# Attention outputs normalised in transposed layout through DRAM, and S^T of two heads into neighbouring banks under one exponential

## What is computed

```python
scores = jnp.einsum('bhqd,bhkd->bhqk', q, k) / jnp.sqrt(jnp.float32(HEAD_DIM))
scores = jnp.where(causal[None, None], scores, neg)
probs = jax.nn.softmax(scores.astype(jnp.float32), axis=-1).astype(x.dtype)
out = jnp.einsum('bhqk,bhkd->bhqd', probs, v)
out = out.transpose(0, 2, 1, 3).reshape(B, S, D_MODEL)
return out @ Wo
```

## Time and profile before

| | |
|---|---|
| three timed runs | 2179.16, 2183.64, 2201.61 us (median 2183.64) |
| profiled execution, own time | 2203.77 us |
| span in its profile | 2202.0 us |
| mean granted TensorE clock | 0.938 |
| TensorE, weight load, VectorE, ScalarE, GpSimd busy | 87%, 42%, 56%, 53%, 41% of the span |

### The profile page before, as it was taken

One profiled execution on the slowest core, in us unless ns is written; L12 is line 12 of the kernel. 1 busy time (PEld: TensorE's weight loads), 2 busy tenths in 40 slices (PEclk: granted clock), 3 DMA queues, 4 the chain that ended last, 5 costly groups with the idle time before them and its releaser, 6 DMA issues.

```text
span 2202.0 us, 37596 instructions
## 1 busy us (share of the span) xinstructions
PE 1912.8 (87%) x12579; PEld 922.6 (42%) x12579; DVE 1236.4 (56%) x2714; ACT 1160.7 (53%) x2592; POOL 904.8 (41%) x1209
## 2 busy tenths in 40 slices
PE   5989999999999999999999999999886888888820
PEld 3544344345444444444444544444332444444410
DVE  3455777656677765658777466787723111222248
ACT  1465577667657766665777766678642122222200
POOL 4744432345442354545433554343214122222248
PEclk9998999999999999999999999999988899999965
DMA  5565332222221122212111122111011999999988
GB/s 179 170 222 172 116 118 84 93 68 92 70 91 53 43 70 71 66 54 85 57 38 37 48 61 61 58 54 38 16 46 34 294 301 283 311 323 293 287 249 289
DMA packets 201642, 280.63 MB, mean 127 GB/s; under 512 B 109783, under 2 KB 109783, under 8 KB 201472
## 3 DMA queue, kind: packets, MB, share of 16 engines
q1 hardware_dynamic: 175152, 239.32, 33.4%
q0 software_dynamic: 24576, 35.07, 6.6%
q10 hardware_dynamic: 1744, 4.06, 0.5%
HBM read 168.85 MB, written 147.46 MB: 144 GB/s over the span
## 4 chain that ended last, share of the span: by engine, by line
PE 62%; DMA 11%; ACT 8%; DVE 7%; issue 5%; SPq 3%; POOL 2%; DVEq 1%; POOLq 1%; ACTq 0%
PE ps L867 11%; PE ps L831 7%; DMA gx<-dispatch_scratch 6%; PE ps L802 6%; ACT pr L1093 5%; PE ps L979 5%; PE ps L851 5%; PE ps L891 5%; PE ps L911 5%; PE ps L1011 3%; PE ps L918 3%; SPq L629 2%; PE ps L933 2%; DVE rmax L1275 2%; DMA qT<-mT 2%
## 5 line engine op out<-in xcount | busy, mean ns | idle before, releaser
L1275 DVE TENSOR_REDUCE rmax<-ps 128x1 f32<-128x512 f32 (+3 forms) x1280 | 735.3, 631 | 251.6 <-PE ps L836 164.3
L1093 ACT ACTIVATE pr<-ps 128x512 f32<-128x512 f32 (+3 forms) x1536 | 623.1, 513 | 169.1 <-PE ps L851 166.8
L831 PE MATMUL ps<-kT,qT 48*128 48x512 f16 (+3 forms) x1536 | 350.4, 337 | 24.5 <-DVE rmax L1275 14.4
L867 PE MATMUL ps<-pr,v_ones 128*32 128x512 f32 (+3 forms) x3072 | 334.7, 527 | 6.9 <-ACT pr L1093 2.8
L1572 POOL TENSOR_SCALAR_AFFINE_SELECT pr<-pr 128x512 f32<-128x512 f32 x256 | 163.8, 642 | 415.3 <-ACT pr L1093 414.7
L851 PE MATMUL ps<-qT,kT 50*128 50x512 f16 (+3 forms) x1536 | 301.7, 338 | 33.5 <-DMA qT<-mT 24.6
L1597 POOL DMA_INDIRECT dispatch_scratch<-x,slot_i x192 | 191.7, 999 | 143.9 <-DVE slot_i L1367 94.9
L1630 POOL DMA_INDIRECT acc_scratch<-eo,etok x64 | 98.8, 1543 | 309.6 <-DVE eo L1417 280.4
L831 PEld LDWEIGHTS ps<-kT,qT 48*128 48x128 f16 x1536 | 106.4, 93 | 274.0 <-ACT pr L1093 93.8
L979 PE MATMUL ps<-gu_sb,gxT 128*128 128x384 f32 x512 | 199.5, 515 | 0.0
L802 PE MATMUL ps<-wqkv_sb,xT 128*128 128x288 f32 (+1 forms) x512 | 181.4, 501 | 4.2 <-ACT xT L1048 4.2
(11 more groups left out here) (147 smaller groups left out, 2596.2 us busy)
## 6 DMA issues: line engine op xcount, KB each, us to landing
gu_sb<-w_gu_dram SPq DMA_DIRECT2D x64, 768.0 KB, 6.6
dn_sb<-w_dn_dram SPq DMA_DIRECT2D x64, 384.0 KB, 8.9
dispatch_scratch<-blank SPq DMA_DIRECT2D x64, 288.5 KB, 4.5
gx<-dispatch_scratch SPq DMA_DIRECT2D x64, 288.5 KB, 5.4
rotated_scratch<-qkv SPq DMA_DIRECT2D x32, 384.0 KB, 2.4
grp<-rotated_scratch SPq DMA_DIRECT2D x32, 384.0 KB, 3.6
xin<-x_dram SPq DMA_DIRECT2D x32, 256.0 KB, 3.2
xres<-x_dram SPq DMA_DIRECT2D x32, 256.0 KB, 2.8
```

Of the source, the lines that this page charges most:

```text
L831: last = pe.matmul(o, qT[it % 2][r:r + SROWS, h // 2, q % QPH * P:(q % QPH + 1) * P], kT[it % 2][r:r + SROWS, kh * HALF:kh * HALF + w], st ...
L867: last = pe.matmul(ps[32 * h:32 * h + 32, bank_of["v", it], c0:HALF], v_ones[it % 2][:, kt, :], pr[k % SLOTS][:, h, 0:HALF - c0], start=kt ...
L1093: act.activation(pr[k % SLOTS][:, h, 0:HALF - c0], ps[:, bank_of["s", it, i, h], 0:HALF - c0], ACT.Exp, scale=factor).then_inc(exp_done, 1)
L1275: dve.tensor_reduce(dst[:, heads[0] % 2, heads[0] // 2:heads[0] // 2 + n, q % QPH], ps[:, bank_of["u", it, u], 0:n * w].rearrange("p (h k) ...
```

## The change

What it does: the outputs of an item stay transposed. The copied bank `raw` (256 KB) is stored to DRAM as it is, and two loads per item bring the value rows into half of a chunk of `anT` and the denominator rows into the same rows of `den`, so that two items fill 128 partitions. VectorE then takes the reciprocal of all 128x512 denominators and multiplies, once for a pair of items, and the output projection reads `anT` directly. `raw_transpose`, `attended_transpose`, `copy_anT` and their waits are gone. S^T of two heads goes into two neighbouring banks, one exponential reads both, and the planner looks for such pairs of banks. Several planner constants are others. The diff, cut to its core (renamed counts and removed tiles are left out):

```diff
-H0 = 0.32
-AHEAD = 4
-RESERVE = 3
+H0 = 0.409
+AHEAD = 3
-ULEAD = -0.186
-ALEAD = 0.066
+ULEAD = -0.628
+ALEAD = 0.047
-CLAG = 0
-CSTEP0 = 0.173
-CSTEP1 = 0.124
+CLAG = 0.057
+CSTEP0 = 0.151
+CSTEP1 = 0.113
...
-                for h in range(REP):
-                    kd = REP * k + h - AHEAD
...
+                for p in range(2):
+                    kd = 2 * k + p - AHEAD
+                    op(s_st, ("st", it, i, p), "pe", n_cols / 2400 + 0.008, t_i,
+                       ("exp", *p_unit(kd // 2), kd % 2) if kd >= 0 else None, ("mr", it), bank=("s", it, i, p))
+                    op(s_exp, ("exp", it, i, p), "act", 0.06 + 2 * n_cols / 1200, t_i, ("st", it, i, p),
+                       ("pv", *p_unit(k - SLOTS)) if k >= SLOTS else None, frees=("s", it, i, p), table="exp")
...
-            op(s_rt, ("rt", it), "pe", 0.45, t_i + 2 * step, ("raw", it), bank=("r", it))
-            op(s_an, ("an", it), "dve", 0.67, t_i + 2.2 * step, ("rt", it), ("as", far) if far is not None else None, frees=("r", it))
-            op(s_as, ("as", it), "sp", 0.06, t_i + 3 * step, ("an", it))
+            op(s_as, ("as", it), "sp", 0.06, t_i + 2 * step, ("raw", it))
+            op(s_nl, ("nl", it), "sp", 0.12, t_i + 3 * step, ("as", it), ("an", it // 2 - 2) if it >= 4 else None,
+               ("wo", it // KVH * QPH - QPH - 1) if it >= 2 * KVH else None)
+            if it % 2:
+                op(s_an, ("an", it // 2), "dve", 1.10, t_i + 5 * step, ("nl", it))
...
-                    need = 1
+                    need = 2 if name[0] == "st" else 1
...
+                    if need == 2:
+                        pairs = [(k, k + 1) for k in free_at if k + 1 in free_at]
+                        if not pairs:
+                            continue
...
+            def store_raw(it):
+                sp.wait_ge(pv_copied, it + 1)
+                sp.dma_start(raw_t[it], raw[it % 2][:]).then_inc(raw_out[it % 2], 16)
+
+            def load_raw(it):
+                sp.wait_ge(raw_out[it % 2], 16 * (it // 2 + 1))
+                if it >= 4:
+                    sp.wait_ge(an_ready, it // 2 - 1)
+                if it >= 2 * KVH:
+                    sp.wait_ge(wo_done, QPH * (it // KVH - 1))
+                rows = slice(ROWT * (it % 2), ROWT * (it % 2) + ROWT)
+                sp.dma_start(anT[it // KVH % 2][rows, it % KVH // 2, :], raw_parts[it, 0]).then_inc(raw_in[it // 2 % 2], 16)
+                sp.dma_start(den[it // 2 % 2][rows, :], raw_parts[it, 1]).then_inc(raw_in[it // 2 % 2], 16)
...
-                pe.matmul(ps[:, bank_of["s", it, i, h], 0:HALF - c0],
-                          kT[it % 2][r:r + BROWS, kt * P:(kt + 1) * P],
-                          qT[it % 2][r:r + BROWS, h // 2, c0:HALF],
-                          start=True, stop=True).then_inc(st_done, 1)
+                for h in range(2):
+                    r = ROWT * h
+                    last = pe.matmul(ps[:, bank_of["s", it, i, pair][h], 0:HALF - c0],
+                                     kT[it % 2][r:r + BROWS, kt * P:(kt + 1) * P],
+                                     qT[it % 2][r:r + BROWS, pair, c0:HALF],
+                                     start=True, stop=True)
+                last.then_inc(st_done, 1)
...
-                pe.wait_ge(anT_copied, n + 1)
+                pe.wait_ge(an_ready, QPH * (n // QPH + 1))
...
-                act.activation(pr[k % SLOTS][:, h, 0:HALF - c0], ps[:, bank_of["s", it, i, h], 0:HALF - c0], ACT.Exp,
+                a, z = bank_of["s", it, i, pair]
+                act.activation(pr[k % SLOTS][:, 2 * pair:2 * pair + 2, 0:HALF - c0],
+                               ps[:, a:z + 1:z - a, 0:HALF - c0], ACT.Exp,
                                scale=factor).then_inc(exp_done, 1)
...
-            def attended(it):
...
-                dve.reciprocal(rden[:], rows[:, :, HD])
+            def attended(pp):
+
+                dve.wait_ge(raw_in[pp % 2], 64 * (pp // 2 + 1))
+                heads = anT[pp // (KVH // 2) % 2][:, pp % (KVH // 2), :]
+                dve.reciprocal(den[pp % 2][:], den[pp % 2][:])
                 dve.drain()
...
+                dve.tensor_tensor(heads, heads, den[pp % 2][:], ALU.mult).then_inc(an_ready, 1)
...
+    raw_d = nc.dram_tensor("raw_scratch", (NI * P, HALF), f32, kind="Internal").ap()
```

More of the change, by code:

```diff
@@ L199, in build @@
                 op(s_stk, ("stk", it, j), "pe", 0.45 * cols / 1024, tpp + (0.3 + 0.05 * j) * dp, ("lo", it),
-                   ("st", far, last_far, REP - 1) if far is not None else None, bank=("k", it, j))
+                   ("st", far, last_far, 1) if far is not None else None, bank=("k", it, j))
                 op(s_stc, ("stc", it, j), "act", 0.05 + cols / 1200, tpp + (0.35 + 0.05 * j) * dp, ("stk", it, j), frees=("k", it, j))
@@ L225, in build @@
                 if diagonal(half, kt):
-                    op(s_mask, ("mask", it, i), "pool", 0.61, t_i, ("exp", it, i, REP - 1))
-                op(s_pv, ("pv", it, i), "pe", 0.04 + n_cols / 600, t_i + 1.2 * step, ("exp", it, i, REP - 1),
+                    op(s_mask, ("mask", it, i), "pool", 0.61, t_i, ("exp", it, i, 1))
+                op(s_pv, ("pv", it, i), "pe", 0.04 + n_cols / 600, t_i + 1.2 * step, ("exp", it, i, 1),
                    ("mask", it, i) if diagonal(half, kt) else None, ("v", it) if i == 0 else None,
-                   ("rt", far) if i == 0 and far is not None else None, bank=("v", it) if i == 0 else None)
@@ L230, in build @@
-            op(s_raw, ("raw", it), "act", 0.48, t_i + 1.2 * step, ("pv", it, NP[half] - 1), ("rt", far) if far is not None else None,
+                   bank=("v", it) if i == 0 else None)
+            op(s_raw, ("raw", it), "act", 0.48, t_i + 1.2 * step, ("pv", it, NP[half] - 1), ("as", far) if far is not None else None,
                frees=("v", it))
-            op(s_rt, ("rt", it), "pe", 0.45, t_i + 2 * step, ("raw", it), bank=("r", it))
-            op(s_an, ("an", it), "dve", 0.67, t_i + 2.2 * step, ("rt", it), ("as", far) if far is not None else None, frees=("r", it))
@@ L340, in run @@
                         continue
-                    if name[0] not in ("st", "pv") and len(free_at) - need + held_s + held_v < RESERVE:
+                    if name[0] not in ("st", "pv") and len(free_at) - need + 2 * held_s + held_v < 3:
                         continue
-                    banks = (min(free_at, key=lambda k: (max(at, free_at[k]), -free_at[k])),)
+                    if need == 2:
+                        pairs = [(k, k + 1) for k in free_at if k + 1 in free_at]
+                        if not pairs:
+                            continue
+                        banks = min(pairs, key=lambda v: (max(at, free_at[v[0]], free_at[v[1]]), -free_at[v[0]] - free_at[v[1]]))
+                    else:
+                        banks = (min(free_at, key=lambda k: (max(at, free_at[k]), -free_at[k])),)
                     at = max([at] + [free_at[k] for k in banks])
```

116 lines of the change are left out of this document (29 added, 87 removed).

## The result

The changed kernel takes 2363.38 us (median of four runs, 2342.64 to 2375.77) against 2187.89 us before (four runs, 2179.16 to 2201.61): 1.0786 times, 95% interval 1.0686 to 1.0887. The forecast was 2139. The profiled execution took 2375.77 us, span 2374.0.

The account below looks back on a forecast made before the run. The prediction took TensorE, 96% busy in the steady attention stage, as the bound. Its terms, -57 - 6 + 37 - 8 - 10 - 1 = -45 us, took the median from 2183.6 to 2139, range 2075 to 2205.

Parts of the forecast that it names:

- Part 3: Stores and loads of the new layout on SyncE's queue: cost taken as 0, as the planner spaces them.
- Part 2: VectorE's reciprocal and product per pair: a 4.3 us block, 1.7 us of it exposed at 0.68 share, +37 us.
- the bound of +96: Upper bound for VectorE's normalisation block: 32 x 3.0 us, bare but for the two score units in hand.
- Part 1: Transposes removed from TensorE: -57 us of chain and -6 us of idle time before them.
- rival C: TensorE's busy time is no bound and other waits fill the holes: about 2184 us, chance 0.16.
- Part 4: Two heads per exponential on ScalarE: -8 us on the path, bounds -43 and +20 to +40.
- Part 5: New planner constants, score units aimed earlier, less TensorE waiting for the transfer into qT: -10 us, bounds 25 either way.
- Part 6: End of the attention stage: last raw copy to first projection 9.5 us (+1.4), later projections -2.5, together -1 us.
- B: VectorE's block holds TensorE at each of 32 pairs: 122 us in place of 37, 2224 us, chance 0.12.

Follow-up runs that it names:

- neither: Changed kernel, same order, with VectorE not waiting for the loads and multiplying by 1 instead of taking the reciprocal: 2188.91 us, stage end 1703.7.
- no_reciprocal: Changed kernel, same order, with VectorE multiplying the denominators by 1 instead of taking their reciprocal: 2248.87 us, ratio 1.0361, stage end 1783.9.
- all_off_pairs: Changed kernel without VectorE's load wait or reciprocal, planner told longer maxima issue and later loads: 2208.29 us, ratio 1.0047, stage end 1721.0.
- all_off: Kernel before plus transposed normalisation only, without VectorE's load wait or reciprocal, planner told longer maxima issue and later loads: 2187.71 us, ratio 0.9988.
- compact: Kernel before plus transposed normalisation, reciprocal on one 128x32 copy spread back through DRAM, planner told measured durations: 2196.57 us, ratio 1.0049, stage end 1735.3.
- other_order: Kernel before with two planner constants moved slightly (ALEAD, CSTEP0), same work in another order: 2208.18 us, ratio 1.0104, stage end 1721.1.
- pairs_only: Kernel before plus S^T in pairs of neighbouring banks, one exponential for two heads and AHEAD 3: 2252.30 us, ratio 1.0421, stage end 1759.0.

## Why the prediction was wrong

- **Part 3, the transfers at 0: the step that failed.** The prediction said that the planner "spaces the two by 2.2 us, hence I take 0". The store landed in 2.0 us by its row; after, the median is 3.1 (4.7 in the chain shown), the load takes 5.9, and the two with their issue 11.2 us. The prediction looked for the cost on SyncE; the larger part fell on VectorE, whose wait for the load it did not price at all. By neither and no_reciprocal it is +80 us of stage, +96 beside the long reciprocal.
- **Part 2, the block: length right, exposure too small.** 4.1 us against 4.3 forecast. The Trainium skill, "VectorE: DVE Perf Modes", section "First, the fixed hardware budget", gives a repeat count of 8, from which 4.4 us were estimated for the reciprocal; it took 3.35, so the reading of that count as 8 cycles per element does not hold here. The slope from the 16-column row stands. But the block costs 78 us of stage and not 37: within the bound of +96, which was the case of two units in hand and no other cover.
- **Part 1, the transposes at -63: nothing was returned.** In neither busy time fell by 50 us and the stage by 4; in all_off_pairs by 34, with the stage 13 later. That is rival C for this part: TensorE 96% busy was not the bound in these orders, as its own waits for others were next. In all_off and compact the step fails in another way, which no rival named: busy time fell by 14 us and not at all, as the other matmuls covered more time. The Trainium skill, "Perfetto Trace Analysis", section "Identifying the Most-Contended Engine", takes weight-load share rather than matmul busy share as the nearer measure. This case is in line with it: 45% of the steady stage, and in neither 50 us off the matmuls bought 4. What spoke against it, that the chain is mostly matmuls, was a poor witness: such a chain names who worked last, not what comes next when that work is gone.
- **Part 4, pairs at -8.** The exponential was sized right (1.02 us for 128x1024 against 1.05), but its saving did not show: +51 alone, outside the bounds of -43 and +40, with longer waits of ScalarE for S^T and of TensorE for banks. On top of the new normalisation pairs and constants gained 24 to 43 us.
- **Part 5, constants at -10 with ±25.** Alone +41, where other_order shows some 13 for a new order as such. The bound of 25 was too narrow, and it was drawn from the waits: they hardly changed, the overlap of the matmuls did.
- **Part 6, the end.** From the last raw copy to the first projection it takes 11.5 us (1795.72 + 0.61 to 1807.85 in the chain), not 9.5; the transfers again.
- **The rivals.** B named the mechanism, VectorE's block holding TensorE, but gave it 0.12 and 2224 us: its 122 us left out the wait for the loads, which the block spends in VectorE's queue as well. With the 174 measured in place of 122 it would have said some 2276, and with nothing for parts 1, 4 and 5 about 2357 (2183.6 + 174). That this lies close to 2363 is no test of the parts: the 174 are counted from a kernel that is level with before.

## What to carry to other kernels

When an edit moves work onto an engine with a fixed order, price what it waits for as part of its length: here 11 us of transfers stood in front of 4 us of arithmetic, and the planner had been given 1.1. Time taken off the busiest engine is only worth what the next waits leave of it; read the waits of second rank, and add them up, before counting the busy time as gain, and allow for a new order in which the matmuls overlap less. An instruction priced by element should be given each value once, and parts measured alone need not add up.

## What the runs showed of the hardware that was not expected

- The reciprocal costs (3353 - 158)/511 = 6.25 ns per column from one to 512 columns, against 158 ns for one; 128x32 took 342 ns, on that line within 10 ns (158 + 31 x 6.25 = 352).
- TensorE does the same work slower after it has stood. In the changed kernel's chain eight projections right after a block of VectorE's took 6.48 us (670.89 on) at a granted clock of 0.57, that is mostly at the lower of its two levels, 1.2 GHz; in the 10.8 us before them TensorE had been busy 4.6. Eight more took 3.63 us from 677.78 on, at 1.00, the level of 2.4 GHz. At the end of the stage before, the first eight took 6.46, at 0.57 too, and eight later ones 3.69. Over the steady stage the granted clock was 0.92 in place of 0.97, and TensorE's total busy time did not fall although 62 us of transposes had gone.
- The expert stage, in which no kernel here differs, took from 352 us (pairs_only) to 404 us (other_order) from its first weight load to its last in the profiled executions. Totals scatter with it, so an effect in the attention stage is better read at that stage's end.
